# Two sixteen-head attention layers of a fused eight-layer kernel joined into one pipeline of sixteen batches

## The chip, the cores and the metric

The kernel runs on one core of a Trainium2 chip. The metric is the device time of one execution, in microseconds (us). Five engines work side by side, each on its own list of instructions in order: TensorE (PE in the rows, PEld for its weight loads), VectorE (DVE), ScalarE (ACT), GpSimd (POOL) and SyncE (SP), which here only issues DMA transfers. They meet at semaphores.

## The reference, cut to what matters

`x` is (8 batches, 256 tokens, 256 features). Eight layers follow one another; each adds its result to `x`. The two that the change touches are the third pair:

```python
x = x + _L2_xattn_ref(_layernorm(x), ctx_1024, ...)   # "a2": q from x, k and v from the context, biases
x = x + _L2_ffn_ref(_layernorm(x), ...)               # "f2": q, k and v from x itself, with a router
# inside _L2_ffn_ref, per head of 16 features:
q_norm = q / norm(q);  q_scaled = (q_norm + query_embedding) * softplus(temperature)
attn = softmax(q_scaled @ k.T / 4);  h = attn @ v
gates = softmax(h @ Wr.T + br)   # 15 experts, the three largest are summed, times 3
sw = softmax(h @ Ws.T + bs)      # 2 values
out = h * (2*sw[0]*sw[0] + 2*sw[1]*3*top3_sum);  return out @ Wp.T + bp
```

Both attentions work on each batch by itself: batch b of `f2` needs batch b of `x` after `a2`, and no other batch.

## The kernel before

`program` calls one function for each layer in the order a0, f0, a1, f1, a2, f2, a3, f3. `attention16` serves a0 (shared keys and values), a2 (`bias=True`) and f2 (`router=True, kv_from_x=True`). Each call opens a block of its own: it clears its semaphores, loads its weights, fills GpSimd's tiles `KP` and `v4` with ones, computes the layer-norm factors of all sixteen token tiles at once (`norm_factors` on VectorE, a square root on ScalarE), and then runs its steps. No engine enters the next block before all have left the last.

A step is a round over eight numbers n = 0..7. At each n come a `score` of the batch three behind, a `max` of the batch two behind, and then the extras of `HEAD_EXTRAS` (a2, a0) or `ROUTED_EXTRAS` (f2), each with the number of batches that it lags: the normalised rows transposed (`xT`), the projections `q`, `k`, `v`, the negated maxima transposed (`neg0`, `neg1`), weighing of values (`weigh0..3`), output transposes (`T0`, `T1`, `aT`) and the output projection `y`. With eight batches and a lag of five there are 13 steps for each layer; in the last five, no new batch enters. All engines walk the same lists. `HEAD_MOVES` and `ROUTED_MOVES` give the order in which SyncE issues the DMAs that carry q, k and the negated maxima through DRAM into `QP` and `KP`; it waits at each until its data is there. The small products share two PSUM buffers (`GP`, a ring in the order of the list), so the use of a buffer waits for whoever reads the use before the last.

`max` is four matmuls into two PSUM tiles `MX[0]` and `MX[1]`, and VectorE reduces each with an instruction of its own (line 806). `score` writes `EX`, which ScalarE turns into exponentials (line 558).

In f2 the query path is: `q` on TensorE, then `square` (bias, square and sum per head on VectorE), a power of -0.5 on GpSimd (line 498), `scale` (one Newton step, factor and embedding on VectorE), transposes `qT`, a split by ScalarE (line 525) and by GpSimd (line 483). The router is `gate` on TensorE, `gate_logits`, one exponential on ScalarE (line 573) and `gate_factor` on VectorE.

Of the kernel before, what the change touches and what calls it, by code (L numbers as in the profile page):

```python
# [20 lines left out]
P = 128  # L21
# [189 lines left out]

def add_to_x(dve, g, b, y):

    xb = g.x[:, bass.ds(b * TT, TT), :]
    op = dve.tensor_tensor(xb, xb, y, ALU.add)
    return op


def next_stats(dve, g, b):
    for t in range(TT):  # L220
        i = b * TT + t
        dve.bn_stats(g.stats[:, bass.ds(i, 1), :].rearrange("p a d -> p (a d)"),
                     g.x[:, bass.ds(i, 1), :].rearrange("p a d -> p (a d)"))
# [32 lines left out]
def at_least(eng, sem, count):  # L256
    if count > 0:
# [10 lines left out]
HEAD_MOVES = [("ctx", -1), ("neg1_out", 3), ("q_in", 1), ("neg1_in", 3), ("k_in", 1), ("q_out", 0), ("neg0_out", 2),  # L268
              ("k_out", 0), ("neg0_in", 2)]
ROUTED_MOVES = [("neg1_out", 3), ("k_in", 1), ("neg1_in", 3), ("q_out", 1), ("q_in", 1), ("neg0_out", 2), ("k_out", 0),  # L270
                ("neg0_in", 2)]


def head_steps(extras):

    steps = []
    for s in range(-1, B + LOOKAHEAD):
        step = []
        for n in range(H // 2):
            step += [(f"score{n}", s - 3), (f"max{n}", s - 2)]  # L280
            step += [(what, s - part) for what, part in extras.get(n, [])]
        steps.append([(what, b) for what, b in step if 0 <= b < B])
    return steps
# [6 lines left out]
def attention16(nc, g, name, w, kv_from_x=False, shared_kv=False, bias=False, router=False):  # L290
# [7 lines left out]
    steps = head_steps(ROUTED_EXTRAS if router else HEAD_EXTRAS)  # L298
    moves = [(what, s - part) for s in range(-1, B + LOOKAHEAD)
             for what, part in (ROUTED_MOVES if router else HEAD_MOVES)  # L300
             if 0 <= s - part < B and not (shared_kv and what in ("k_out", "k_in"))
             and not (kv_from_x and what == "ctx")]
# [3 lines left out]
    column = lambda h: 8 * (h // 8) + 4 * (h % 2) + (h // 2) % 4  # L306

    with ExitStack() as ctx:
# [6 lines left out]
        wq, wv, wo = sb("wq", [P, KD, D]), sb("wv", [P, KD, VH * 16]), sb("wo", [P, KD, D])  # L315
        wk = sb("wk", [P, KD, P if shared_kv else D])
        xn = sb("xn", [P, TT, D])
        xnT = sb("xnT", [P, KD, S])
        kvT2 = None if kv_from_x else sb("kvT", [P, 2, KD, S])
# [15 lines left out]
        bk = sb("bk", [P, KD])  # L335
        if bias:
            bq = sb("bq", [P, KD])
            bv, bo = sb("bv", [P, D]), sb("bo", [P, D])
        if router:
            bqt, qe = sb("bqt", [P, D]), sb("qe", [P, D])  # L340
            sp_t = sb("sp_t", [P, 4, H])
            spq = sb("spq", [P, H])
            half = sb("half", [P, TT * H])
            qtm, qsq = sb("qtm", [P, TT, D]), sb("qsq", [P, TT, D])
            qn = sb("qn", [P, 3, TT * H])
            wr, br = sb("wr", [P, KD, H + 1]), sb("br", [P, H + 1])
            lg, le = sb("lg", [P, TT, 24]), sb("le", [P, TT, 24])
            top, sm = sb("top", [P, TT, 8]), sb("sm", [P, TT, 8])
        ps = lambda n, k: [ctx.enter_context(nc.psum_tensor(f"{name}_{n}{i}", [P, TT, S], F32)) for i in range(k)]
        GP, MX, EX, OT = ps("gp", 2), ps("mx", 2), ps("ex", 2), ps("ot", 2)  # L350

        first_in, weights_in = sem("first_in"), sem("weights_in")
# [10 lines left out]
        q_sums, q_roots, q_scaled, softplus, act_step = (sem(n) for n in (  # L363
            "q_sums", "q_roots", "q_scaled", "softplus", "act_step"))
        gate_in, gate_exp = sem("gate_in"), sem("gate_exp")
        gp_full, gp_read = [sem(f"gp_full{i}") for i in range(2)], [sem(f"gp_read{i}") for i in range(2)]
        mx_full, mx_read = [sem(f"mx_full{i}") for i in range(2)], [sem(f"mx_read{i}") for i in range(2)]
# [15 lines left out]
        def scored(eng, b):  # L383
            eng.wait_ge(ex_full[1], 8 * (b + 1))

        row_of = lambda v: w[v].rearrange("(a n) -> a n", a=1)
        first_loads = [(wq[:], w["wq"].rearrange("(k p) n -> p k n", p=P)),
                       (wk[:], w["wk"].rearrange("(k p) n -> p k n", p=P)), (bk[:], w["bk"])]
        loads = [(wv[:], w["wv"].rearrange("(k p) n -> p k n", p=P)), (wo[:], w["wo"].rearrange("(k p) n -> p k n", p=P))]
        if bias:  # L390
            loads += [(bv[:], row_of("bv").broadcast_to([P, D])), (bo[:], row_of("bo").broadcast_to([P, D]))]
        if bias and not router:
            first_loads += [(bq[:], w["bq"])]
        if router:
            first_loads += [(bqt[:], row_of("bq").broadcast_to([P, D])), (qe[:], row_of("qe").broadcast_to([P, D])),
                            (sp_t[:, 0, :], row_of("temp").broadcast_to([P, H]))]
            loads += [(wr[:], w["wr"].rearrange("(k p) n -> p k n", p=P)),
                      (br[:], row_of("br").broadcast_to([P, H + 1]))]
        first_all, all_in = 16 * len(first_loads), 16 * len(loads)
# [5 lines left out]
        def _(sp):  # L405
# [3 lines left out]
            def load_rest():  # L409
                for dst, src in loads:  # L410
                    sp.dma_start(dst, src).then_inc(weights_in, 16)

# [37 lines left out]
            if kv_from_x:  # L450
# [21 lines left out]
        def _(pool):  # L472
            pool.memset(KP[:].bitcast(F32), 1.0).then_inc(fixed, 1)
            pool.memset(v4[:], 1.0).then_inc(fixed, 1)
            if router:
                pool.memset(half[:], -0.5)
                pool.drain()
# [8 lines left out]
            for step in steps:  # L486
                for what, b in step:
                    if what == "norm":
                        if b >= 1:
                            full(pool, "xT", b - 1)  # L490
                        normalise(pool, g, b, xn, xn_ready)
                    elif what == ("qT" if router else "q"):
# [3 lines left out]
                    elif what == "square":  # L496
                        pool.wait_ge(q_sums, b + 1)
                        pool.tensor_tensor(qn[:, 2], qn[:, 0], half[:], ALU.pow).then_inc(q_roots, 1)
                    elif what == "v" and bias:
                        if b == 0:  # L500
                            pool.wait_ge(weights_in, all_in)
                        pool.wait_ge(xn_ready, b + 1)
                        xb = g.x[:, b * TT:(b + 1) * TT, :]
                        pool.tensor_tensor(xb, xb, bo[:].rearrange("p (a n) -> p a n", a=1).broadcast_to([P, TT, D]),
# [3 lines left out]
        def _(act):  # L508
            norm_sqrt(act, g, sqrt_in, sqrt_out)
            act.wait_ge(first_in, first_all)  # L510
            if router:
# [19 lines left out]
            for step in steps:  # L531
                for what, b in step:
                    bank = gp.slot((what, b)) if (what, b) in gp.place else None
                    if what == "xT":
                        if kv_from_x and b >= 1:
# [3 lines left out]
                    elif what == "q" and not router:  # L539
                        split_rows("q", b, qf, qs, q_split, q_out, bq if bias else None)  # L540
                    elif what == "qT":
                        split_rows("qT", b, qf, qs, q_split, q_out, None)
# [2257 lines left out]
```

## Time and profile before

| | us |
|---|---|
| median of 3 runs | 2100.21 (2098.96 to 2108.5) |
| the profiled execution, its own time | 2091.46 |
| its span in the trace | 2089.7 |
| TensorE busy | 1607.8 |
| VectorE busy | 996.2 |
| ScalarE busy | 674.8 |
| GpSimd busy | 512.9 |

The rows below are of that one execution. Its own time is 8.75 us under the median of the runs. In the rows `a_` names a tile of an attention layer and `f_` one of an f layer; between 969.2 and 1507.7 us of the span these are a2 and f2. The granted clock of TensorE is a share of 2.4 GHz. A row of the windows gives the stretch and its length, then busy us with the count of instructions for PE, PEld, DVE, ACT and POOL, then the granted clock, the share of time the DMA engines were busy, and GB/s. In a timeline, a group of several instructions shows its start and its length, and in brackets how long the engine was idle before it, and for whom.

### The profile page before, as it was taken

The numbers are of one execution on the slowest core, as the hardware profiler recorded it, in microseconds if no ns is written. First come the engines' busy times: TensorE is split into PE (matmuls) and PEld (weight loads), VectorE is DVE, ScalarE is ACT, GpSimd is POOL, SyncE is SP. The second block draws the span as 40 slices with busy tenths as digits, with TensorE's granted clock in tenths as the row PEclk, the third lists the DMA queues.
The fourth block names the chain that finished last, engine by engine and source line by source line (L and its number), as shares of the span: only waits on it lengthen the run. The fifth ranks groups of instructions, "written<-read, shape, count | busy, mean of one in ns | idle before, by whom it ended". The sixth has DMA issues, their size and how long they took to land. (4 is left out here: it accounts for less than half of the span.)

```text
span 2089.7 us, 33375 instructions
## 1 busy us (share of the span) xinstructions
PE 1607.8 (77%) x12250; PEld 1235.2 (59%) x12250; DVE 996.2 (48%) x2190; ACT 674.8 (32%) x1408; POOL 512.9 (25%) x583
## 2 busy tenths in 40 slices
PE   4898775905888519981699746888699999999976
PEld 2565654804566418871466434655478888888766
DVE  2675262524454422113366446776426554455542
ACT  1464342302555101111366413434332222222111
POOL 2110043052444020005331064431042223222110
PEclk8798797957999659995799967988799999999986
DMA  4230553435644258852756034442110000000001
GB/s 135 68 83 18 185 213 105 135 91 153 141 112 92 75 204 295 301 197 86 166 130 133 3 85 108 103 92 53 44 55 7 6 7 1 6 6 2 1 7 41
DMA packets 89430, 195.54 MB, mean 94 GB/s; under 512 B 13536, under 2 KB 62176, under 8 KB 80704
## 3 DMA queue, kind: packets, MB, share of 16 engines
q1 hardware_dynamic: 76352, 173.07, 28.9%
q0 software_dynamic: 4608, 12.59, 1.8%
q10 hardware_dynamic: 8320, 7.87, 1.1%
q8 instruction: 96, 1.57, 0.3%
q14 instruction: 54, 0.44, 0.1%
HBM read 136.47 MB, written 57.02 MB: 93 GB/s over the span
## 5 line engine op out<-in xcount | busy, mean ns | idle before, releaser
L806 DVE TENSOR_REDUCE a_sb_mx<-a_mx 128x2 f32<-128x512 f32 x256 | 164.8, 686 | 97.7 <-PE a_mx L634 97.4
L1161 DVE RECIPROCAL a_sb_rden<-a_ot 128x256 f32<-128x256 f32 x64 | 112.1, 1752 | 146.6 <-PE a_ot L1047 146.5
L558 ACT ACTIVATE a_sb_probs<-a_ex 128x512 f32<-128x512 f32 x256 | 139.2, 598 | 103.9 <-PE a_ex L655 103.3
L230 PE MATMUL a_gp<-g_ident,a_sb_xn 128*128 128x128 f32 x128 | 25.1, 329 | 163.0 <-POOL a_sb_xn L206 80.0
L230 PEld LDWEIGHTS a_gp<-g_ident,a_sb_xn 128*128 128x128 f32 x128 | 16.9, 165 | 167.5 <-DMA a_sb_bo<-a_bo 70.9
L806 DVE TENSOR_REDUCE f_sb_mx<-f_mx 128x2 f32<-128x512 f32 x128 | 82.2, 684 | 36.7 <-PE f_mx L634 36.3
L558 ACT ACTIVATE f_sb_probs<-f_ex 128x512 f32<-128x512 f32 x128 | 69.5, 597 | 71.5 <-PE f_ex L655 71.4
L990 ACT ACTIVATE a_sb_probs<-a_sc 128x512 f32<-128x512 f32 x64 | 38.2, 597 | 167.9 <-PE a_sc L1035 111.7
L959 POOL TENSOR_SCALAR_AFFINE_SELECT a_sb_probs<-a_sb_probs 128x256 f32<-128x256 f32 x128 | 49.2, 409 | 164.9 <-ACT a_sb_probs L991 164.8
L655 PE MATMUL a_ex<-a_sb_QP,a_sb_KP 49*128 49x256 f32 x512 | 68.1, 343 | 24.8 <-ACT a_sb_probs L558 21.3
L952 POOL TENSOR_TENSOR a_sb_q_lo<-a_sb_whole,a_sb_q_hi 128x512 fp32r<-128x512 f32 x32 | 40.7, 1271 | 180.0 <-ACT a_sb_q_hi L981 180.0
L2488 PE MATMUL f_hb<-f_sb_xsT,f_sb_wb 128*128 128x128 f32 x640 | 76.0, 281 | 10.9 <-ACT f_sb_xsT L2441 10.9
L2488 PEld LDWEIGHTS f_hb<-f_sb_xsT,f_sb_wb 128*128 128x128 f32 x640 | 74.3, 196 | 13.1 <-issue 6.6
L980 ACT ACTIVATE a_sb_whole<-a_gp 128x512 f32<-128x512 f32 x64 | 38.3, 598 | 134.5 <-PE a_gp L999 134.5
L655 PEld LDWEIGHTS a_ex<-a_sb_QP,a_sb_KP 49*128 49x128 f32 x512 | 42.2, 197 | 63.9 <-issue 40.2
L634 PE MATMUL a_mx<-a_sb_KP,a_sb_QP 48*128 48x256 f32 x512 | 62.7, 322 | 17.4 <-DVE a_sb_mx L806 16.3
L668 PE MATMUL a_ot<-a_sb_probs,a_sb_v 128*32 128x256 f32 x1024 | 74.1, 410 | 0.0
L2602 DVE TENSOR_SCALAR f_sb_hT<-f_hb,f_sb_wb 128x128 f32<-128x128 f32 x80 | 22.5, 344 | 105.3 <-PE f_hb L2488 105.3
L1336 POOL TENSOR_SCALAR_AFFINE_SELECT a_sb_sim<-a_sb_sim 128x256 f32<-128x256 f32 x128 | 49.9, 418 | 89.0 <-ACT a_sb_sim L1390 89.0
L2497 PE MATMUL f_yb<-f_sb_wb,f_sb_hT 128*128 128x256 f32 x320 | 70.7, 379 | 0.0
L1146 DVE TENSOR_REDUCE a_sb_mx<-a_sc 128x2 f32<-128x256 f32 (+1 forms) x128 | 62.1, 544 | 11.6 <-PE a_sc L1020 11.6
L2497 PEld LDWEIGHTS f_yb<-f_sb_wb,f_sb_hT 128*128 128x128 f32 x320 | 60.0, 190 | 7.7
(427 smaller groups left out, 3929.5 us busy)
## 6 DMA issues: line engine op xcount, KB each, us to landing
f_sb_wb<-f_w SPq DMA_DIRECT2D x20, 2052.0 KB, 11.3
a_sb_kvT<-ctxT SPq DMA_DIRECT2D x32, 256.0 KB, 3.5
a_q_moved<-a_sb_qs SPq DMA_DIRECT2D x16, 512.0 KB, 3.5
a_sb_QP<-a_q_moved SPq DMA_DIRECT2D x32, 256.0 KB, 4.7
f_x_slots<-f_sb_zero SPq DMA_DIRECT2D x1, 6144.0 KB, 20.1
f_sb_xs<-f_x_slots SPq DMA_DIRECT2D x20, 256.0 KB, 2.8
f_y_slots<-f_sb_ys ACTq DMA_DIRECT2D x20, 256.0 KB, 2.6
a_sb_QP<-a_q_moved SPq DMA_DIRECT2D x32, 128.0 KB, 5.0
```

What stands on the lines that cost most here:

```text
L230: op = pe.transpose(out[:, k, t * P:(t + 1) * P], xn[:, t, k * P:(k + 1) * P], g.ident[:])
L558: act.activation(probs[:, group % 3, 2 * (u % 2) + par], EX[par][:], ACT.Exp, scale=scale)\
L634: op = pe.matmul(MX[par][:, t, :], QP[at:at + R, b % 3, u, t * P:(t + 1) * P], KP[at:at + R, b % KB, u % KM, :], start=True, stop=True)
L655: op = pe.matmul(EX[par][:, t, :], KP[at:at + R + 1, b % KB, u % KM, t * P:(t + 1) * P], QP[at:at + R + 1, b % 3, u, :], start=True, stop= ...
L668: op = pe.matmul(OT[c // 2][32 * j:32 * j + 32, c % 2, :], v4[:, b % 4, t, (4 * c + j) % VH, :], probs[:, (4 * b + c) % 3, j, t, :], start ...
L806: dve.tensor_reduce(mx[:, :, column(2 * u + par)], MX[par][:], AX.X, ALU.max, negate=True)\
L959: op = pool.affine_select(later, later, [[0, 2], [1, P]], ALU.is_ge, 0.0, base=0, channel_multiplier=-1)
L1146: op = dve.tensor_reduce(mx[:, t, 2 * i:2 * i + 2], SC[pair][:, :, t, 0:(t + 1) * P], AX.X, ALU.max, negate=True)
L1161: dve.reciprocal(rden[:, n], OT[n][:, 1, :])
L1336: op = pool.affine_select(later, later, [[0, 2], [1, P]], ALU.is_ge, 0.0, base=0, channel_multiplier=-1)
L2488: op = pe.matmul(HB[j % 2][c // (FC // 2)][:, c % (FC // 2), :], w1(j, k, c), xsT[:, j, k, :], start=(k == 0), stop=(k == KD - 1))
L2497: op = pe.matmul(YB[j % 2][:, 0], hT[:, j, c, :], w2(j, c), start=(c == 0), stop=(c == FC - 1))
```

## The change

`attention16` takes a list of layers and runs a2 and f2 as one pipeline of sixteen batches: batches 0 to 7 are a2's, 8 to 15 f2's. The weights of both have tiles of their own; f2's large ones are loaded behind a2's. `norm_factors` runs once, for a2. For batches 8 to 15 GpSimd computes the layer-norm factors itself, batch by batch (`batch_norm_factors`), after `y` of the batch eight before has given the new statistics.

```diff
-    elif s == "a2":
-        attention16(nc, g, s, w, bias=True)
-    elif s == "f2":
-        attention16(nc, g, s, w, bias=True, kv_from_x=True, router=True)
+    elif s == "a2":
+        layers = [(sub(io, n + "_"), n == "f2") for n in ("a2", "f2") if n in stages]
+        attention16(nc, g, s, layers)
```
```diff
+def batch_norm_factors(eng, g, b, ln):
+    at = slice(b * TT, (b + 1) * TT)
+    st = lambda i: g.stats[:, at, i]
+    eng.tensor_tensor(ln[:, 0, :], st(1), st(4), ALU.add)
...
+    root_guess(eng, g.rstd[:, at], ln[:, 3, :])
+    for _ in range(3):
+        root(eng, g.rstd[:, at], ln[:, 3, :], g.rstd[:, at], ln[:, 4, :])
```
`root_guess` is one operation on the bits, `root` four operations with a drain after each.
```diff
-ROUTED_EXTRAS = {0: [("neg1", 3), ("xT", 0), ("weigh3", 4), ("y", 5)], 1: [("q", 0), ("square", 0), ("out1", 4)],
-                 2: [("weigh0", 3), ("T0", 4), ("T1", 4)], 3: [("k", 0)], 4: [("neg0", 2), ("weigh1", 3), ("aT", 4)],
-                 5: [("scale", 0), ("gate", 4), ("v", 0), ("out0", 3), ("norm", -1)], 6: [("weigh2", 3), ("gexp", 4)],
-                 7: [("qT", 0), ("factor", 4)]}
+ROUTED_EXTRAS = {0: [("neg1", 3), ("xT", 0), ("weigh3", 4), ("y", 5)], 1: [("q", 0), ("out1", 4), ("norm", -1)],
+                 2: [("square", 0), ("weigh0", 3), ("T0", 4), ("T1", 4)], 3: [("k", 0), ("sums", 0)],
+                 4: [("neg0", 2), ("weigh1", 3), ("aT", 4), ("roots", 0)], 5: [("gate", 4), ("out0", 3)],
+                 6: [("weigh2", 3), ("gexp", 4), ("v", 0), ("scale", 0)], 7: [("qT", 0), ("factor", 4)]}
```
In a routed step the work moves so: the square goes from VectorE to ScalarE; the inverse root goes from one power on GpSimd and a Newton step on VectorE to fourteen small operations on GpSimd; adding the embedding becomes the bias of ScalarE's split of `qT`; the copies of the negated maxima go from VectorE to ScalarE.
```diff
-                        pool.tensor_tensor(qn[:, 2], qn[:, 0], half[:], ALU.pow).then_inc(q_roots, 1)
+                        root_guess(pool, qn[:, 3], qn[:, 0])
+                        for _ in range(3):
+                            root(pool, qn[:, 3], qn[:, 0], qn[:, 3], qn[:, 1])
+                        by_token = lambda a: a.rearrange("p (t h) -> p t h", t=TT)
+                        pool.tensor_tensor(by_token(qn[:, 2]), by_token(qn[:, 3]), ..., ALU.mult).then_inc(q_rooted, 1)
```
The router's exponential on ScalarE becomes six instructions, three for each token tile, each of which also gives the sum of its row; the three largest are found in the logits, before the exponential, and twelve small VectorE operations are left of nineteen.
```diff
-                        act.activation(le[:, :, 0:H + 1], lg[:, :, 0:H + 1], ACT.Exp).then_inc(gate_exp, 1)
+                        for t in range(TT):
+                            act.activation(le[:, t, 0:H - 1], lg[:, t, 0:H - 1], ACT.Exp, bias=neg_top[:, t, 0:1],
+                                           accum_out=sums[:, t, 0:1])
...
```
In all three layers served by `attention16`, a0 too, the two maxima tiles become one, which VectorE reduces with one instruction:
```diff
-                        for par in range(2):
-                            dve.wait_ge(mx_full[par], 8 * b + u + 1)
-                            dve.tensor_reduce(mx[:, :, column(2 * u + par)], MX[par][:], AX.X, ALU.max, negate=True)\
-                               .then_inc(mx_read[par], 1)
+                        dve.wait_ge(mx_full, 2 * (8 * b + u + 1))
+                        pair = mx[:].rearrange("p t (i g h) -> p g t i h", i=2, g=2)[:, :, :, u // 4, u % 4]
+                        dve.tensor_reduce(pair, MX[:], AX.X, ALU.max, negate=True).then_inc(mx_read, 1)
```
On SyncE, in a routed step, the second half of the negated maxima comes back (`neg1_in`) ahead of the keys (`k_in`) instead of behind them. Five small loads of f2 now stand in a2's first group, which the first q waits for.

## Rows read from the trace of the kernel before

**Rows 1.** Windows: a2 until its last batch enters, its tail, f2 likewise.
```profile
969.20:1136.60 167.40, 132.73 (x982) 91.76 (x982) 87.63 (x152) 81.50 (x168) 58.21 (x42) 0.87 0.58 139
1136.60:1205.20 68.60, 51.70 (x459) 32.10 (x458) 34.30 (x68) 31.66 (x59) 0.00 (x0) 0.89 0.14 25
1205.20:1421.80 216.60, 154.99 (x1038) 106.66 (x1038) 141.26 (x299) 80.56 (x159) 101.86 (x50) 0.79 0.40 96
1421.80:1507.70 85.90, 67.01 (x499) 42.22 (x498) 47.44 (x165) 33.34 (x65) 1.27 (x1) 0.80 0.12 26
```

**Rows 2.** Windows, same columns: one full step of a2, one full step of f2.
```profile
1115.40:1136.60 21.20, 20.35 (x181) 13.77 (x180) 14.13 (x26) 13.68 (x28) 3.78 (x3) 1.00 0.56 127
1391.60:1421.80 30.20, 26.42 (x193) 17.63 (x192) 21.75 (x57) 13.50 (x27) 9.24 (x4) 0.83 0.37 88
```

**Rows 3.** What TensorE waited for in f2: us in total, times, longest.
```profile
PE f_mx L634 <- DVE f_sb_mx L806: 27.7, 21, 4.5
PE f_gp L230 <- DVE f_sb_qtm L733: 18.1, 2, 9.1
```

**Rows 4.** Timeline of TensorE in a full step of f2: start, duration, what.
```profile
1383.40 1.06 PE L587 MATMUL f_gp<-f_sb_wr,f_sb_oT 128*128 128x17 f32 x8
1384.31 1.97 PE L587 MATMUL f_gp<-f_sb_wv,f_sb_xnT 128*128 128x256 f32 x8
...
1390.53 0.50 PE L634 MATMUL f_mx<-f_sb_KP,f_sb_QP 48*128 48x256 f32 x4 [1.99 <-DVE f_sb_mx L806]
1390.96 0.66 PE L230 MATMUL f_gp<-g_ident,f_sb_qtm 128*128 128x128 f32 x4
...
1397.03 3.78 PE L587 MATMUL f_gp<-f_sb_wo,f_sb_oT 128*128 128x256 f32 x8 [0.52 <-DVE f_sb_negT L813]
1400.74 0.80 PE L655 MATMUL f_ex<-f_sb_QP,f_sb_KP 49*128 49x256 f32 x4
```

**Rows 5.** Timeline of TensorE in a full step of a2.
```profile
1124.40 0.40 PE L634 MATMUL a_mx<-a_sb_KP,a_sb_QP 48*128 48x256 f32 x4
1124.73 1.99 PE L580 MATMUL a_gp<-a_sb_kvT,a_sb_wk 128*128 128x256 f32 x8
```

**Rows 6.** VectorE in f2, groups by shape: busy us, mean ns, idle before.
```profile
L806 DVE TENSOR_REDUCE f_sb_mx<-f_mx 128x2 f32<-128x512 f32 x128 | 82.2, 684 | 36.7 <-PE f_mx L634 36.3
L813 DVE CAST f_sb_negT<-f_gp 8x256 fp32r<-8x256 f32 x16 | 6.4, 403 | 0.1
L717 DVE TENSOR_TENSOR f_sb_qsq<-f_sb_qtm 128x512 f32<-128x512 f32 x8 | 5.5, 692 | 0.7
L1189 DVE TENSOR_TENSOR f_sb_qn<-f_sb_qn 128x32 f32<-128x32 f32 x8 | 4.0, 502 | 11.2 <-POOL f_sb_qn L498 11.2
L726 DVE TENSOR_TENSOR f_sb_qn<-f_sb_qn,f_sb_spq 128x32 f32<-128x32 f32 x8 | 1.6, 202 | 0.6
```

**Rows 7.** GpSimd in the whole span, groups by shape.
```profile
L498 POOL TENSOR_TENSOR f_sb_qn<-f_sb_qn,f_sb_half 128x32 f32<-128x32 f32 x8 | 43.6, 5454 | 69.7 <-DVE f_sb_qn L719 69.7
L483 POOL TENSOR_TENSOR f_sb_qs<-f_sb_qf,f_sb_qs 128x512 fp32r<-128x512 f32 x8 | 10.2, 1271 | 43.8 <-ACT f_sb_qs L525 43.8
L1932 POOL TENSOR_TENSOR f_sb_s_hT<-f_sb_s_act,f_sb_s_lin 128x256 f32<-128x256 f32 x8 | 6.3, 789 | 36.8 <-ACT f_sb_s_lin L2012 36.8
L476 POOL MEMSET f_sb_half<- 128x32 f32 x1 | 0.1, 143 | 0.0
```

**Rows 8.** ScalarE in f2, groups by shape.
```profile
L528 ACT ACTIVATE f_sb_ks<-f_gp,f_sb_bk 128x256 fp32r<-128x256 f32 x16 | 6.7, 480 | 0.0
L573 ACT ACTIVATE f_sb_le<-f_sb_lg 128x34 f32<-128x34 f32 x8 | 1.9, 234 | 5.5 <-DVE f_sb_lg L746 5.5
L558 ACT ACT_TABLE_LOAD x1 | 1.3, 1283 | 0.0
```

**Rows 9.** Timeline of VectorE at f2's start, beside GpSimd's memset.
```profile
1205.78 4.74 DVE L177 TENSOR_SCALAR g_ln_mean<-g_ln_mean 128x16 f32<-128x16 f32 x1
```

**Rows 10.** Timeline of SyncE's queue at f2's start, one of twelve loads.
```profile
1206.73 0.43 SPq L407 DMA_DIRECT2D f_sb_bqt<-f_bq  x1
```

More of the change, by code:

```diff
@@ L280, in head_steps, with __init__, attention16 @@
             step += [(f"score{n}", s - 3), (f"max{n}", s - 2)]
-            step += [(what, s - part) for what, part in extras.get(n, [])]
-        steps.append([(what, b) for what, b in step if 0 <= b < B])
-    return steps
+            for which, extras in ((True, ROUTED_EXTRAS), (False, HEAD_EXTRAS)):
+                step += [(what, s - part) for what, part in extras.get(n, []) if of_layer(s - part, which)]
+        steps.append([(what, b) for what, b in step if 0 <= b < n_b])
+        moves += [(what, s - part) for what, part, kinds in MOVES
+                  if 0 <= s - part < n_b and routed[(s - part) // B] in kinds]
+    return steps, moves
 def number(what):
     return int("".join(c for c in what if c.isdigit()))
-def attention16(nc, g, name, w, kv_from_x=False, shared_kv=False, bias=False, router=False):
+class Layer:
+    def __init__(self, i, w, router):
+        self.w, self.router, self.first = w, router, i * B
+def attention16(nc, g, name, layers, shared_kv=False):
     io = g.io
@@ L297, in attention16 @@
     scale = 0.25
[L298 to L302, printed above, removed]
+    bias = not shared_kv
+    L = [Layer(i, w, router) for i, (w, router) in enumerate(layers)]
+    NB = B * len(L)
+    of = lambda b: L[b // B]
+    routed = lambda b: of(b).router
+    steps, moves = head_steps([l.router for l in L])
+    moves = [(what, b) for what, b in moves if not (shared_kv and what in ("k_out", "k_in"))]
     flat = [u for step in steps for u in step]
@@ L392, in attention16 @@
[L392 to L399, printed above, removed]
+        by_k = lambda a: a.rearrange("(k p) n -> p k n", p=P)
@@ L748, in gate_logits @@
-                op.then_inc(gate_in, 1)
+                dve.tensor_scalar(neg_top[:, :, 0], top[:, :, 0], -1.0, None, ALU.mult)
+                dve.drain()
+                dve.sem_inc(gate_in, 1)
             def gate_factor(b):
-                dve.wait_ge(gate_exp, b + 1)
-                for i, (lo, hi) in enumerate(((0, H - 1), (H - 1, H + 1))):
-                    dve.tensor_reduce(sm[:, :, i], le[:, :, lo:hi], AX.X, ALU.add)
-                for t in range(TT):
-                    dve.max(top[:, t, :], le[:, t, 0:H - 1])
+                dve.wait_ge(gate_exp, b - of(b).first + 1)
@@ L776, in _ @@
                     bank = gp.slot((what, b)) if (what, b) in gp.place else None
-                    if what == "square":
-                        square_q(b)
+                    if what == "q" and routed(b):
+                        bias_q(b)
+                    elif what == "sums":
+                        sum_q(b)
                     elif what == "scale":
```

314 lines of the change are left out of this document (184 added, 130 removed).

## The prediction

> **What bounds it now.** I read the windows of the stretch first. From 969.2 us to 1507.7 us, 538.5 us, the chip works on the two layers, in four parts: a2 until its last batch is in (167.4 us), a2's tail of five steps in which no batch enters (68.6), f2 until its last batch is in (216.6), f2's tail (85.9) [rows 1]. The reader is to see TensorE: 52 us of work in a tail of 68.6, and 155 us in f2's 216.6, at a granted clock of 0.79. Everything outside this stretch stays as it is, but for a0, below.
>
> Then one full step of each layer [rows 2]. A step of a2 takes 21.2 us, and TensorE is busy for 20.35 of them at its upper level, 2.4 GHz all the way. This layer is bound by TensorE. A step of f2 takes 30.2 us. VectorE is busy for 21.75 of them, TensorE for 26.42, but at a mean clock of 0.83: part of that work ran at the lower level, 1.2 GHz.
>
> The waits say why. TensorE's largest wait in f2 is for the reduction of the maxima on VectorE, 27.7 us, and then for the scaled query [rows 3]. In the timeline of the step the 1.99 us before the max at 1390.53 are such a wait; VectorE was busy with Newton step, scaling, embedding and router in front of that reduction. Soon after it the clock is down: the output projection at 1397.03 takes 3.71 us to the next score, where a product of the same size takes 1.93 in a2 [rows 4, 5]. So f2 loses to VectorE's order of work, and then a second time by the clock.
>
> **Part 1, the join.** a2's tail and f2's start now overlap. Batch 8 needs the statistics of batch 0, which `y` gives in step 4; its `norm` is in step 7, three steps later, so nothing waits there. The stretch becomes: a2's first part as it is, 167.4; eight steps with routed batches entering; one tail of a routed layer. What is removed is 68.6 + 216.6 + 85.9 = 371.1 us [rows 1]; I now price what takes its place.
>
> **Part 2, a full routed step (steps 12 to 15).** TensorE: the 20.35 us of an a2 step, plus what only f2 has, the gate with 0.91 (1383.40 to 1384.31) and the transposes of q with 0.6 [rows 2, 4]: 21.9 us. With the 0.85 us that an a2 step already idles: 22.7.
>
> VectorE: of its 21.75 us it loses the square (0.69), the added embedding (the same shape, 0.69), two copies of negated maxima (0.81), and five small operations of Newton step and factor; these go from 0.20 to 0.50 each, 1.0 to 2.5 us, I take the middle, 1.75 [rows 6]. The router loses seven small operations of 0.15 to 0.20, about 1.2. That leaves 16.6 us for 24. The joined reduction saves nothing I can count: two of 0.684 that overlap against one of 1024 elements. If the element rate holds it costs about 1.2 instead of 1.3 us; if a reduction over two tiles gained nothing, 1.37. I take it as equal, here and in a0: 0.1 us either way on each of 64 pairs a layer is 6 us of VectorE's work in a layer, most of it in its idle time.
>
> Three waits are new or left. After the last `v` product, VectorE copies v and scales q (0.69 each, the shape of the square [rows 6]) and hands over twice (0.1 each), 1.6 us, before `qT` can start; TensorE has one score and one max in between, 0.33 each [rows 5]: 0.9 us idle. The next step's first max waits for the reduction behind that scaling: 0.25. Then `xT` waits for its PSUM buffer until ScalarE has written q twice, now with a bias and so in four instructions of 0.48 [rows 8], 1.6 us less the matmuls in between: 0.5. Sum 1.65, so the step is 22.7 + 1.65 = 24.3 us, if the clock stays up.
>
> Steps 8 to 11 have routed q work but no gate yet (it lags four): 22.7 - 0.9 + 0.9 = 22.7 us.
>
> **Part 3, GpSimd's small operations.** The trace has no short arithmetic on GpSimd. From below: a memset of 128x32 took 0.143. From above: a subtraction on 512 elements took 1.27, and one on 32 can't take more; the power with 5.45 is another operation. The nearest two-input rows are 0.789 for 256 and 1.27 for 512; their line gives 0.31 + 0.06 for 32, so 0.37 us [rows 7]. I take that, drain included. The chain that matters is in the middle of the step: ScalarE splits k in 1.5 us after TensorE's k, GpSimd takes 1.27 for the rest, then come fourteen root operations, 5.2 us, to 8.0. VectorE wants the result behind v. k closes n = 3 and v n = 6, so this is three eighths of a step later, 9.1. In total GpSimd has in a step the fourteen and 21 of `batch_norm_factors` (13.0 us), two for normalising and three for the splits and the bias, which I put at 1.27 each (6.3): 19.3 of 24.3. It is hidden, with 1.1 us to spare in the chain. At 0.45 us each the cover is gone and each further 0.1 us costs 1.4 us a step.
>
> The Trainium skill speaks against this part: its page Perfetto Trace Analysis, Optimizing GPSIMD Operations and the note on offloading, says to prefer other engines, because GpSimd and VectorE share an SBUF port, so that moving work between those two may not help. The trace has a case: a 128x16 operation of VectorE took 4.74 us beside a memset of GpSimd [rows 9]. What that would make of the sum is a rival below.
>
> **Part 4, the rest.** ScalarE takes on the square (0.6), two copies (0.4 each), five more instructions for the router (0.23 each, or up to 0.48 with the sums) and two more splits: 13.5 + 3 to 4.5, or at most 18 of 24 [rows 2, 8]; the six router exponentials stand behind score 6, beside weigh2 and v, 3 us of TensorE. Hidden; if not, 1 to 2 us a step. SyncE: `neg1_in` moves ahead of four issues of about 0.45; its data is needed at n = 4, ten us later, no gain; `k_in` needs to land before the next step. Nothing. At the start, five more loads in the first group (0.43 each, 2.2 us of queue [rows 10]) land while GpSimd fills its tiles: 0, at worst 2. The exponential and logarithm for softplus run in the same shadow.
>
> **Part 5, the tail.** It lies between a2's 68.6 and f2's 85.9 [rows 1]: gate and router are in it, the slow clock (0.80) and VectorE's excess partly not. I take the middle, 77.
>
> **Sum.** 4 x 22.7 + 4 x 24.3 + 77 = 265 us in place of 371.1: 106 us less. The profiled execution, 2091.5, would become 1985.5; the median of the runs, 8.75 us higher, becomes 2100.2 - 106 = 1994 us.
>
> **Rivals.**
> A. The clock falls in the routed steps as it does now. For it: bubbles of 0.9 and 0.5 us remain behind `v`, where 1.99 preceded the fall. Against: a0 and a2 keep 2.4 GHz with small waits. It costs what the slow piece costs now, about 3.3 us in steps 12 to 15 and 1.3 before them, and the tail is 86: 4 x 24 + 4 x 27.6 + 86 = 292, 79 less: 2021 us.
> B. GpSimd sets the step, with about 0.6 us for a small operation: 35 x 0.6 + 6.3 = 27.3, so 28 us with its waits; 8 x 28 + 86 = 310, 61 less: 2039.
> C. The port: what VectorE hands to GpSimd costs it as much in waits. 1.75 us a step come back on the path, 14 us in all: 2008.
> D. ScalarE has to exchange its function table for the square. The row of such a load is 1.283 [rows 8]; two in each routed step, half hidden: 10 us, 2004 to 2014. Copies and exponentials alternate without one now; for a square there is no row.
> E. Slower. A small GpSimd operation with its drain takes 1.27 us, as much as a large one. Then GpSimd needs 35 x 1.27 + 6.3 = 51 us a step: 8 x 51 + 86 = 494, 123 more: 2223. It decides from the point where a step reaches (371 - 86) / 8 = 35.6 us, 0.84 us for each operation. Speaking against it: the larger one has sixteen times the elements.
> F. Better than forecast: the waits hide and the tail is a2's. 8 x 22.7 + 68.6 = 250, 121 less: 1979.
>
> **How the numbers follow.** Forecast 0.48; A 0.18; B 0.08; C 0.08; D 0.05; E 0.03; F 0.10. Their neighbourhoods overlap. The predicted time is the forecast's, 1994. The range goes from F, lowered by the 8.75 us by which single executions differ, 1971, to just short of B, 2034; left out are E, most of B and what lies below F. 0.5% is 10.5 us, about what a measurement of this kernel can tell from no change. Only E, or a mishap I did not list, gives a time above 2090: slower 0.03, same 0.01, faster 0.96.
>
> **What would show it.** Between about 969 and 1402 us one stretch without a hole; steps 8 to 11 near 22.7 us and 12 to 15 near 24.3, at a clock of 1.0; the max waits of 2 us gone and one near 0.9 us before `qT`; small GpSimd operations spaced 0.3 to 0.4 us and the last root before VectorE's copy of v; a tail under 80 us. The forecast is wrong if VectorE waits for GpSimd before scaling, if GpSimd's spacing passes 0.45, if table loads appear behind squares, or if the clock in the routed steps is near 0.85.

## The result, and the profile after

| | before | changed |
|---|---|---|
| median, us | 2102.89 (2098.96 to 2108.5, 4 runs) | 1991.82 (1987.47 to 1997.49, 4 runs) |
| profiled execution, own time | 2091.46 | 1997.49 |
| its span | 2089.7 | 1995.7 |
| TensorE, VectorE busy | 1607.8, 996.2 | 1571.1, 942.9 |
| ScalarE, GpSimd busy | 674.8, 512.9 | 694.5, 523.9 |

The ratio is 0.9472 (95% interval 0.9437 to 0.9506): 104 to 118 us of 2102.9 are gone. The forecast was 1994. The two profiled executions lie on opposite sides of their medians, so that between the traces only 94 us are to be seen; a later trace of the same changed kernel (experiment 3) has a span of 1988.3, and so shows 101.

First the windows of the changed kernel, with the columns of [rows 1]: until a2's last batch is in, steps 8 to 11, steps 12 to 15, the tail (its last 0.6 us, in which TensorE is done, are left out); then step 9, step 10 and step 14 by themselves. Step 8 is the first in which a batch of f2 enters; steps 8 to 11 also carry the rest of a2, and step 14 is a full routed step.

```profile
969.20:1133.60 164.40, 130.79 (x982) 90.42 (x983) 85.22 (x107) 84.72 (x173) 68.10 (x83) 0.87 0.63 150
1133.60:1228.20 94.60, 84.16 (x739) 57.77 (x738) 66.51 (x81) 57.51 (x119) 49.70 (x142) 0.98 0.48 108
1228.20:1325.10 96.90, 89.75 (x761) 60.69 (x760) 68.13 (x120) 63.19 (x168) 47.99 (x137) 0.96 0.49 111
1325.10:1412.50 87.40, 67.48 (x499) 42.51 (x498) 40.20 (x108) 40.85 (x116) 1.28 (x1) 0.79 0.13 26
1156.80:1181.90 25.10, 22.29 (x187) 15.18 (x186) 17.01 (x21) 14.27 (x29) 15.25 (x44) 0.93 0.45 107
1181.90:1205.00 23.10, 20.58 (x185) 14.18 (x184) 16.69 (x20) 14.36 (x30) 11.93 (x37) 1.00 0.51 116
1274.90:1299.30 24.40, 22.33 (x195) 15.25 (x194) 17.49 (x33) 16.12 (x43) 13.65 (x40) 1.00 0.47 111
```

The stretch takes 443.9 us (969.2 to 1413.1) where it took 538.5, 94.6 less, which is the whole difference of the spans. The hole between the layers is gone, and the clock of the routed steps is 0.96 to 0.98 where it was 0.79 [rows 1]. The steps 8 to 15 are 23.2, 25.1, 23.2, 23.2, 21.4, 25.3, 24.4 and 25.8 us. VectorE is busy for 17.5 us of step 14, TensorE for 22.3 of 24.4. In f2's full step before, the two were 21.8 and 26.4 of 30.2 [rows 2]. TensorE now fills 92% of a full routed step with work at its upper clock level, where it filled 96% of a step of a2.

TensorE's waits of the changed kernel from 1133 to 1402 us (total, times, longest), to set beside [rows 3]:

```profile
PE a_ex L739 <- ACT a_sb_probs L639: 15.3, 21, 1.6
PE a_gp L252 <- DVE a_sb_qtm L810: 11.4, 8, 1.7
PE a_ot L752 <- ACT a_sb_probs L639: 2.1, 1, 2.1
PE a_mx L718 <- DVE a_sb_mx L880: 1.6, 2, 0.8
```

The wait for the maxima has gone from 27.7 us to 1.6. The wait for the scaled query was 18.1 us in two places; now there is one of about 1.4 us in every routed step. The largest total is now for ScalarE's exponentials; 10.0 of it lie between 1330 and 1412 us, in the tail.

TensorE's timeline in step 9 of the changed kernel, beside [rows 4], and behind it the end of step 8:

```profile
1172.62 1.99 PE L675 MATMUL a_gp<-a_sb_wv,a_sb_xnT 128*128 128x256 f32 x8
...
1175.88 0.40 PE L718 MATMUL a_mx<-a_sb_KP,a_sb_QP 48*128 48x256 f32 x4
1177.94 0.63 PE L252 MATMUL a_gp<-g_ident,a_sb_qtm 128*128 128x128 f32 x4 [1.65 <-DVE a_sb_qtm L810]
1178.40 3.53 PE L675 MATMUL a_gp<-a_sb_wo,a_sb_oT 128*128 128x256 f32 x8
```
```profile
1154.51 0.63 PE L252 MATMUL a_gp<-g_ident,a_sb_qtm 128*128 128x128 f32 x4 [1.38 <-DVE a_sb_qtm L810]
1154.97 1.89 PE L675 MATMUL a_gp<-a_sb_wo,a_sb_oT 128*128 128x256 f32 x8
```

The `y` (the output projection) at 1178.40 takes 3.53 us behind a wait of 1.65; in step 8 the same product takes 1.89 behind a wait of 1.38. The clock still falls here in steps 9, 13 and 15 (granted 0.93 over each of them, 1.00 over step 10), and stays at its upper level in the other five; step 12 has no `y` at all.

Near the end of step 12, VectorE first and then GpSimd in the same microseconds:

```profile
1247.01 0.69 DVE L871 TENSOR_TENSOR a_sb_v<-a_gp,a_sb_bv 128x512 f32<-128x512 f32 x1 [1.44 <-PE a_gp L675]
1247.62 1.26 DVE L810 TENSOR_TENSOR a_sb_qtm<-a_sb_qtm,a_sb_qn 128x512 f32<-128x512 f32 x1
1248.80 1.21 DVE L880 TENSOR_REDUCE a_sb_mx<-a_mx 128x4 f32<-128x1024 f32 x1
```
```profile
1246.08 0.22 POOL L1271 TENSOR_SCALAR a_sb_qn<-a_sb_qn 128x32 f32<-128x32 f32 x1 [0.16 <-issue]
1246.44 0.25 POOL L1273 TENSOR_TENSOR a_sb_qn<-a_sb_qn 128x32 f32<-128x32 f32 x1
1246.84 0.25 POOL L566 TENSOR_TENSOR a_sb_qn<-a_sb_qn,a_sb_spq 128x32 f32<-128x32 f32 x1
1247.05 1.28 POOL L573 TENSOR_TENSOR g_x_all<-g_x_all,a_sb_bo 128x512 f32<-128x512 f32 x1
```

The fourteen small operations of GpSimd start 0.36 to 0.42 us apart. The last of them ends at 1247.09, as VectorE begins its copy of v, and the scaling that needs it starts at 1247.62: in time, with 0.5 us to spare. Right behind it GpSimd starts a large operation, the output bias, and VectorE's scaling beside it takes 1.26 us, where the copy of the same shape, beside the same operation, took 0.69.

In steps 8 to 10 the roots are late instead: VectorE waits for them, three times, 1.5 us in all. The scaling of step 8, then GpSimd's addition beside it:

```profile
1152.62 1.75 DVE L810 TENSOR_TENSOR a_sb_qtm<-a_sb_qtm,a_sb_qn 128x512 f32<-128x512 f32 x1 [0.37 <-POOL a_sb_qn L566]
```
```profile
1152.54 1.28 POOL L573 TENSOR_TENSOR g_x_all<-g_x_all,a_sb_bo 128x512 f32<-128x512 f32 x1
```

Here the scaling takes 1.75 us, in step 12 it takes 1.26, and in both it ends 0.55 us behind the end of the addition.

### The profile page after: what moved, and what is told of

It is laid out like the page before. It is cut to its first block and busy times, and to the rows that moved or that the text cites. A ratio compares the mean times of both kernels' runs of the same rounds, so it can differ in the third digit from the quotient of the medians.

```text
span 1995.7 us, 33445 instructions
## 1 busy us (share of the span) xinstructions
PE 1571.1 (79%) x12250; PEld 1213.6 (61%) x12250; DVE 942.9 (47%) x1858; ACT 694.5 (35%) x1533; POOL 523.9 (26%) x852
## 3 DMA queue, kind: packets, MB, share of 16 engines
q1 hardware_dynamic: 76496, 172.94, 30.5%
## 5 line engine op out<-in xcount | busy, mean ns | idle before, releaser
L880 DVE TENSOR_REDUCE a_sb_mx<-a_mx 128x4 f32<-128x1024 f32 x192 | 234.7, 1223 | 114.9 <-PE a_mx L718 112.6
L639 ACT ACTIVATE a_sb_probs<-a_ex 128x512 f32<-128x512 f32 x384 | 208.8, 598 | 157.6 <-PE a_ex L739 157.3
L252 PE MATMUL a_gp<-g_ident,a_sb_xn 128*128 128x128 f32 x160 | 31.0, 325 | 165.3 <-POOL a_sb_xn L206 80.8
L739 PE MATMUL a_ex<-a_sb_QP,a_sb_KP 49*128 49x256 f32 x768 | 99.2, 335 | 32.3 <-ACT a_sb_probs L639 29.6
L752 PE MATMUL a_ot<-a_sb_probs,a_sb_v 128*32 128x256 f32 x1536 | 112.4, 414 | 2.1 <-ACT a_sb_probs L639 2.1
L739 PEld LDWEIGHTS a_ex<-a_sb_QP,a_sb_KP 49*128 49x128 f32 x768 | 61.0, 191 | 87.0 <-issue 58.0
L718 PE MATMUL a_mx<-a_sb_KP,a_sb_QP 48*128 48x256 f32 x768 | 90.4, 313 | 14.1 <-DVE a_sb_mx L880 13.3
L718 PEld LDWEIGHTS a_mx<-a_sb_KP,a_sb_QP 48*128 48x128 f32 x768 | 64.1, 201 | 25.6 <-DVE a_sb_mx L880 16.6
L539 POOL TENSOR_TENSOR a_sb_qs<-a_sb_qf,a_sb_qs 128x512 fp32r<-128x512 f32 x24 | 30.6, 1274 | 184.4 <-ACT a_sb_qs L594 97.2
L752 PEld LDWEIGHTS a_ot<-a_sb_probs,a_sb_v 128*32 128x32 f32 x1536 | 42.1, 114 | 40.1 <-issue 14.1
```

Source lines behind the costliest of these rows:

```text
L252: op = pe.transpose(out[:, k, t * P:(t + 1) * P], xn[:, t, k * P:(k + 1) * P], g.ident[:])
L639: act.activation(probs[:, group % 3, 2 * (u % 2) + par], EX[par][:], ACT.Exp, scale=scale)\
L718: op = pe.matmul(MX[:, par, t, :], QP[at:at + R, b % 3, u, t * P:(t + 1) * P], KP[at:at + R, b % KB, u % KM, :], start=True, stop=True)
L739: op = pe.matmul(EX[par][:, t, :], KP[at:at + R + 1, b % KB, u % KM, t * P:(t + 1) * P], QP[at:at + R + 1, b % 3, u, :], start=True, stop= ...
L752: op = pe.matmul(OT[c // 2][32 * j:32 * j + 32, c % 2, :], v4[:, b % 4, t, (4 * c + j) % VH, :], probs[:, (4 * b + c) % 3, j, t, :], start ...
L880: dve.tensor_reduce(pair, MX[:], AX.X, ALU.max, negate=True).then_inc(mx_read, 1)
```

## The experiments

Each was timed against the kernel before in the same series and on the same chip. There were three series: experiments 1 and 2 with the first run of 3 (median of the kernel before: 2099.82); the first run of 4 with all of 5, on another chip (2105.99); the second runs of 3 and 4 with 6, on the first chip again (2103.04). The changed kernel itself was timed in the first and the third; in the second only the ratio to the kernel before can be compared. The theory under test is the prediction's: the join fills the tail, and the rework of the routed step takes VectorE's excess away.

**1. The rework without the join, and the join without the rework.** In the first, the two layers stay two calls:

```diff
-                layers = [(sub(io, n + "_"), n == "f2") for n in ("a2", "f2") if n in stages]
-                attention16(nc, g, s, layers)
+                attention16(nc, g, s, [(w, False)])
+            elif s == "f2":
+                attention16(nc, g, s, [(w, True)])
```

> The changed routed steps, but a2 and f2 as two calls of the function, each with its own block, fill and tail. Theory (two parts, each worth something by itself): the steps of f2 that carry everything fall from 30.2 us to about 24.4, there are three or four such steps, and the maxima waits go: the stretch of the two layers becomes about 515 us from 538.5, the time about 2078 us, 20 to 30 us under the kernel before. Rival (the join is all of it, the rework only undoes what the join would have cost): within 5 us of the kernel before. Second rival (the rework is all of it and the join only hides a short fill): about 2010 us.

In the second, the routed step goes back to its old order and old owners inside the joined pipeline (square, Newton step, embedding, router and negated maxima on VectorE, the power on GpSimd, `neg1_in` behind `k_in`); GpSimd's `batch_norm_factors` and the joined reduction stay.

```diff
-                        root_guess(pool, qn[:, 3], qn[:, 0])
-                        for _ in range(3):
-                            root(pool, qn[:, 3], qn[:, 0], qn[:, 3], qn[:, 1])
...
+                        pool.tensor_tensor(qn[:, 2], qn[:, 0], half[:], ALU.pow).then_inc(q_rooted, 1)
```

> One pipeline of sixteen batches, but the routed step as it was: power on GpSimd, Newton step, square, embedding, router and copies of negated maxima on VectorE, old order of extras and of DMAs. Only the layer-norm factors per batch and the joined reduction stay from the change. Theory: steps with everything take 30 us as in f2 before, the four mixed ones about 24.5, the tail 86: the stretch is 164 + 219 + 86 = 469 us, about 70 us under the kernel before, so 2032 us. Rival (join is all): 1992 us, as the changed kernel. Rival (the join brings nothing without the rework): above 2080.

Measured: rework alone 2064.74 (ratio 0.9833, 0.9798 to 0.9868), 35 us gained, where 2078 was expected; join alone 2027.8 (0.9629, 0.9589 to 0.9669), 72 gained, where 2032 was expected. Both together gained 101 in the same series (2099.82 to 1998.95, experiment 3). The windows of f2 in the first:

```profile
1194.00:1470.90 276.90, 207.75 (x1536) 139.10 (x1536) 149.92 (x271) 136.14 (x353) 84.19 (x154) 0.84 0.36 83
```

and of the routed steps in the second:

```profile
1134.30:1354.00 219.70, 186.90 (x1496) 124.28 (x1496) 151.87 (x289) 106.37 (x210) 127.77 (x196) 0.91 0.42 96
```

f2 alone falls from 302.5 us (216.6 + 85.9 [rows 1]) to 276.9, its full steps from as much as 30.5 to between 22 and 26. The join alone leaves steps of up to 30.5 us, with VectorE busy for 151.9 of 219.7. So the two parts together pay nearly the sum of what each pays alone (101 against 107): one takes a tail away, the other shortens steps that are there in either case. Of the two, the join is worth twice as much.

**2. The router alone undone.** `gate_logits`, the one exponential and `gate_factor` as before, all else changed.

```diff
-                        for t in range(TT):
-                            act.activation(le[:, t, 0:H - 1], lg[:, t, 0:H - 1], ACT.Exp, bias=neg_top[:, t, 0:1],
-                                           accum_out=sums[:, t, 0:1])
...
+                        act.activation(le[:, :, 0:H + 1], lg[:, :, 0:H + 1], ACT.Exp).then_inc(gate_exp, 1)
```

> The changed kernel with the router part undone: one exponential on ScalarE, sums and maxima by small VectorE operations. Theory A (ScalarE is the waiting place in the tail): the six exponentials with their six accumulator reads hold ScalarE 1.7 us in front of the exponentials of score 7, where TensorE waits 1.63 us in each tail step against 0.71 in the kernel before, and then its clock falls; undone, the tail is 3 to 6 us shorter, steps 12 to 15 change by under 1 us each: 2 to 6 us faster than the changed kernel. Theory B (VectorE's seven saved operations carry the step): steps 12 to 15 get 1 to 1.5 us longer each, the kernel 4 to 6 us slower.

Measured 1994.12 (0.9488, 0.9455 to 0.9521), with steps of 23.2, 25.1, 23.2, 23.1, 21.5, 25.4 and 24.4, those of the changed kernel within 0.1. So theory B is refuted: seven small operations less on VectorE lie in its idle time. Theory A is not. The median is 4.8 us under that of the changed kernel in the same series (1998.95, experiment 3), inside the 2 to 6 us that it asked for, but the intervals of the two ratios overlap. The tail of the trace, all but its last 0.6 us:

```profile
1325.80:1407.50 81.70, 64.52 (x499) 41.11 (x498) 44.94 (x143) 35.19 (x72) 1.27 (x1) 0.79 0.13 28
```

TensorE is idle for 17.2 us of it, where it was idle for 19.9 in the changed kernel's at the same clock. The router's rework gained nothing, and may have cost some 3 us in the tail.

**3. The changed kernel again**, unchanged, in the first series and in the third.

> The changed kernel itself on the same chip, for the comparisons: 1992 us within 0.3%.

> The changed kernel on the same chip and in the same rounds, a third trace of its tail, which took 88.0 and 83.3 us in two: again between these if it is the clock's chance; 1992 us, a ratio near 0.949.

Measured 1998.95 (1990.17 to 2005.07), 0.35% above the 1992 expected, and 1993.73 (1991.29 to 1995.24), with stretches of 437.3 and 443.1 us. Steps 8 to 14 repeat within 0.1 us of the first trace. What lies behind them does not: in the first of these traces step 15 takes 24.3 us and the tail 83.3, in the second 25.8 and 88.0, as in the trace above. The tail of the shorter one:

```profile
1319.30:1402.50 83.20, 63.00 (x499) 40.44 (x498) 40.21 (x108) 41.18 (x116) 1.28 (x1) 0.82 0.13 27
```

TensorE is idle for 20.2 us of it, and for 19.9 us of the 87.4 above. What differs is how long the same 499 matmuls take, 63.0 against 67.5 us, at a clock of 0.82 against 0.79.

**4. The output bias later.** GpSimd's addition of the output bias moves, in routed steps, from `v` to behind its split of q, away from VectorE's scaling.

```diff
-                 6: [("weigh2", 3), ("gexp", 4), ("v", 0), ("scale", 0)], 7: [("qT", 0), ("factor", 4)]}
+                 6: [("weigh2", 3), ("gexp", 4), ("v", 0), ("scale", 0)], 7: [("qT", 0), ("factor", 4), ("bias", 0)]}
...
-                    elif what == "v" and bias:
+                    elif bias and what == ("bias" if routed(b) else "v"):
```

> The changed kernel with GpSimd's addition of the output bias moved, in routed steps, from right behind the roots to behind the split of q. Theory (shared port): the scaling of q on VectorE took 1.26 us instead of 0.69 because it ran beside that addition of 1.27 us; moved, the scaling takes 0.69 to 0.75, the wait before the transposes of q falls from 1.38 to about 0.8 us in eight steps, 4 to 5 us, and more if the clock then stays up in steps 9, 13 and 15: 1984 to 1988 us. Rival (the scaling is slow by itself, its access pattern has two strides): no change, 1992.

> The late bias again, with more rounds: its trace had the eight steps about 8 us shorter and the first part 4 us longer, where the code is the same. Theory (the first part's 4 us are a chance of where TensorE's clock falls in the fill): the first part is 164.4 again, the kernel 5 to 8 us under the changed one, a ratio to the kernel before of about 0.944. Rival (the later addition delays something there): the first part stays at 168.

Line 810, the scaling, in the first of these (nanoseconds: least, median, most), and TensorE at the end of step 12:

```profile
L810 DVE TENSOR_TENSOR a_sb_qtm<-a_sb_qtm,a_sb_qn x8: 681/681/694, 1150.2 to 1310.9; 128x512 f32<-128x512 f32 x8
```
```profile
1240.64 0.63 PE L252 MATMUL a_gp<-g_ident,a_sb_qtm 128*128 128x128 f32 x4 [0.80 <-DVE a_sb_qtm L810]
```

The same line in the changed kernel:

```profile
L810 DVE TENSOR_TENSOR a_sb_qtm<-a_sb_qtm,a_sb_qn x8: 1252/1320/1746, 1152.6 to 1323.2; 128x512 f32<-128x512 f32 x8
```

The median of the scaling falls from 1.32 to 0.68 us, and the wait from 1.38 to 0.80, in steps 8 to 10 to 0.6 or less; the steps 8 to 11 fall to 22.1, 22.4, 22.1 and 22.6. This shows that GpSimd's addition beside it is what stretched the scaling. How, the timelines of the changed kernel's three traces say: in all 24 scalings there the end lies 0.54 to 0.56 us behind the end of the addition, whether the scaling started 0.07 or 0.60 us after it. It looks like a wait until the addition is over, not like two operations that share a rate. In the total the gain is hard to see: 1991.84 against 1993.73 of the changed kernel, five executions of each (ratios 0.9471, 0.9454 to 0.9489, and 0.9481, 0.9463 to 0.9499), so 2 us, where 5 to 8 were expected. The stretch is 434.2 us in the second trace and 438.5 in the first, against 437.3 to 443.9 in the three of the changed kernel. In the first trace the part before step 8 took 168.2 us, with the clock at 0.84 instead of 0.87, and in the second 163.9, in the same code: that was chance. The earlier run gave 0.946 (0.9422 to 0.9497); it leaves out one execution of 4891.5 us, for which I have no explanation.

**5. Three single parts.** Two maxima tiles and two reductions again:

```diff
-                        dve.wait_ge(mx_full, 2 * (8 * b + u + 1))
-                        pair = mx[:].rearrange("p t (i g h) -> p g t i h", i=2, g=2)[:, :, :, u // 4, u % 4]
-                        dve.tensor_reduce(pair, MX[:], AX.X, ALU.max, negate=True).then_inc(mx_read, 1)
+                        for par in range(2):
+                            dve.wait_ge(mx_full[par], 8 * b + u + 1)
+                            dve.tensor_reduce(mx[:, :, column(2 * u + par)], MX[par][:], AX.X, ALU.max, negate=True)\
+                               .then_inc(mx_read[par], 1)
```

> The changed kernel with two maxima tiles and two reductions again. Theory: the joined reduction is what shortened a2's first part from 167.4 to 164.4 us, by 0.06 us of VectorE for each max where its wait stands on the path; undone, that part is 167 again, a0 gets 1 to 3 us longer, steps 8 to 15 up to 0.5 each: 5 to 9 us slower than the changed kernel. Rival (the first part got shorter by its start and the order of DMAs): no change within 2 us.

Its first part, with the columns of [rows 1]:

```profile
972.60:1140.20 167.60, 133.06 (x986) 91.93 (x988) 88.33 (x156) 84.62 (x173) 68.13 (x85) 0.87 0.62 147
```

167.6 us against 164.4, and a full step of a2 21.2 to 21.3 against 21.0: the joined reduction gives 3 us there. The part as a whole can move by 4 us without a cause in the code (experiment 4), but the full steps don't: the last four before step 8 are 21.2 to 21.3 us in both traces with two tiles and 21.0 in those with one, the last three of them even in that odd trace. Steps 8 to 15 did not get longer: 190.3 us, where the changed kernel took 189.8 to 191.5. The total, 2003.14 (0.9507, 0.9475 to 0.9538), overlaps with the changed kernel's; a time doesn't resolve it.

The negated maxima copied by VectorE:

```diff
-                    elif what.startswith("neg") and not routed(b):
+                    elif what.startswith("neg"):
```

> The changed kernel with the copies of the negated maxima of f2 back on VectorE. Theory: two copies of 0.40 us a step on an engine busy for 17 of 24, in places (n = 0 and 4) where TensorE has long products: under 1 us a step either way, and ScalarE is freed by 0.37 in the tail; within 4 us of the changed kernel. Rival (VectorE is the bound of the routed step): 0.8 us a step and the clock, 8 us slower or more.

Measured 1997.4 (0.9481, 0.9449 to 0.9513), steps as in the changed kernel: worth nothing that can be measured.

Five Newton steps on GpSimd for the roots of q, eight more operations in the chain that was just in time:

```diff
-                        for _ in range(3):
+                        for _ in range(5):
                             root(pool, qn[:, 3], qn[:, 0], qn[:, 3], qn[:, 1])
```

> The changed kernel with five Newton steps for the root of q on GpSimd instead of three, eight small operations more. Theory (the roots end just when VectorE wants them): 8 x 0.38 = 3.0 us later, of which the copy of v hides 0.5 at most; the wait before the transposes of q grows from 1.38 to about 3.9 us, the clock falls more often: 8 x 2.5 = 20 us or more, 2012 to 2025 us. Rival (GpSimd has slack, the wait is v's copy and the scaling alone): no change.

Measured 2035.04 (0.9665, 0.9619 to 0.9711), beyond the 2012 to 2025 expected, with TensorE's waits from 1130 to 1460 us headed by

```profile
PE a_gp L252 <- DVE a_sb_qtm L810: 34.9, 8, 4.8
```

4.4 us in each routed step for 1.4. The eight operations at 0.38 us are 3.0, less 0.5 of slack; the scaling adds 0.4, since it now starts together with the output bias each time and takes 1.73 us. The eight steps grow by 4.6 us each in the mean (228.2 us for 191.5), so 1.7 us a step come on top of the wait; the slower clock (0.89 over these steps for 0.97) is part of it, how much was not separated. With a slack of 0.5 us at most, the price is 1.5 times what is added (4.6 for 3.0).

Inside the joined pipeline the whole rework was worth 29 us (2027.8 against 1998.95). The router and the copies of the negated maxima have no measurable share in that. Square, roots, embedding and the order of extras and DMAs were undone only all together, and which of them carries the gain is not shown.

**6. The scaling ahead of v**, with the late output bias of experiment 4; VectorE waits there for the roots before it copies v.

```diff
-                 6: [("weigh2", 3), ("gexp", 4), ("v", 0), ("scale", 0)], 7: [("qT", 0), ("factor", 4)]}
+                 6: [("weigh2", 3), ("gexp", 4), ("scale", 0), ("v", 0)], 7: [("qT", 0), ("factor", 4), ("bias", 0)]}
```

> The late bias of the run before, and VectorE scales q ahead of its copy of v instead of behind it. Theory: the roots end as v's product ends, so the scaling starts 0.5 us earlier; the wait before the transposes of q falls from 0.80 to about 0.25 us, steps 12 to 15 to 23.2, the clock stays at 2.4 GHz in all eight; the stretch behind a2's first part is 4 us shorter than with the late bias alone, 10 to 12 shorter than in the changed kernel: 1981 to 1986 us. Rival (the roots are the bound now): the wait moves to VectorE and v's copy with it, no gain over the late bias alone.

TensorE at the end of step 12 of it:

```profile
1240.62 0.63 PE L252 MATMUL a_gp<-g_ident,a_sb_qtm 128*128 128x128 f32 x4 [0.29 <-DVE a_sb_qtm L810]
```

Measured 1987.54 (1982.16 to 1989.45; 0.9449, 0.9428 to 0.9469), stretch 431.1 us. All five executions lie under the changed kernel's five in that series (from 1991.29). It is the fastest version found, 6 us or 0.3% under the changed kernel by the medians; the intervals of the ratios just overlap. It stays short of the 1981 to 1986 us expected. About 2 us of what the shorter wait gives is taken back: the wait for the maxima is now 3.9 us in all, for 1.6. And the clock did not stay up in all eight steps: steps 9 and 10 took 23.4 us each at 0.93.

## Why the prediction was right

- **The join, right.** A tail and a start taken away; alone it gives 72 us. Nothing waits where the layers meet: in steps 8 to 11 TensorE's only listed waits are for the scaled query and for ScalarE's exponentials.
- **The first part, 164.4 for 167.4.** "I take it as equal" was wrong here. The joined reduction takes 1.22 us where the pair takes two of 0.69, and a2 has use for the difference, 0.2 to 0.3 us in each full step (experiment 5), although VectorE is idle for a third of such a step. That `max` waits for the reader of its tile is the likely way, but the list of waits of a full step of a2 names no wait for it.
- **Steps 8 to 11, 22.7 forecast; 23.2, 25.1, 23.2, 23.2.** The wait before the transposes was put at 0.9 and is 1.38 or more: the scaling was priced at 0.69 without its neighbour. Experiment 4 shows the 0.58 us. This is rival C's mechanism at a third of the price that the rival gave it. The Trainium skill, GPSIMD Engine Reference, Specifications, gives GpSimd's SBUF interfaces as shared with VectorE, with contention for VectorE operations that have two SBUF inputs. The trace agrees: the scaling has two and is stretched, the copy of v has one and PSUM, and takes 0.69. TensorE also waits 1.2 us a step for ScalarE's exponentials (4.7 us in the four), for which the sum had nothing but a2's idle time of 0.85; and in step 9 the clock falls.
- **Steps 12 to 15, 24.3 forecast; 21.4, 25.3, 24.4, 25.8.** The mean, 24.2, is right, but by errors that cancel. Step 12 is short because it has no `y`: a2's list has it at the end of the step four later, f2's at the start of the step five later, and the sum left that out. Steps 13 and 15 are long because the clock falls behind the wait that ends the step before them. And of the three waits in the sum, 0.9, 0.25 and 0.5, the first is 1.4 us, while the other two hardly came: no wait for the maxima before the tail, and 0.7 us in all behind `xT`'s buffer.
- **Rival A in part.** Three of eight steps (in one trace two) still lose the clock, 1.4 to 1.7 us of TensorE's time each. The wait ahead of `y` is 1.38 before step 13, which loses the clock, and 1.38 in step 8, which keeps it: the wait alone doesn't decide, and what does stays open. With the late bias and no wait there at all, step 9 kept the clock in one trace (22.4 us) and lost it in the other (23.4 us), where the product of `v` took 3.68 us behind a wait of 1.00 for ScalarE.
- **The tail, 88.0 for 77 (83.3 in one trace of three), the largest error.** The middle between a2's and f2's tail was taken as if the fall of the clock came from VectorE's excess. That excess is gone (40 us busy of 87), and the tail is f2's still: 20 us idle, where f2's had 18.9 and a2's 16.9 [rows 1], and the rest is matmuls at a clock of 0.79. A tail under 80 us, which the prediction named as a sign of being right, came in no trace. TensorE's largest wait there is for ScalarE's exponentials; that too few batches are in flight to fill the gap is argued. A reader can check one such wait; ScalarE's timeline of the changed kernel,

```profile
1346.55 0.31 ACT L655 ACTIVATE a_sb_le<-a_sb_lg,a_sb_neg_top 128x15 f32<-128x15 f32 x1
1346.75 0.20 ACT L655 ACTIVATION_READ_ACCUMULATOR a_sb_le<-a_sb_lg,a_sb_neg_top 128x1 f32 x1
...
1348.16 0.19 ACT L659 ACTIVATION_READ_ACCUMULATOR a_sb_le<-a_sb_lg,a_sb_neg_top 128x1 f32 x1
1348.25 1.06 ACT L639 ACTIVATE a_sb_probs<-a_ex 128x512 f32<-128x512 f32 x2
```

and TensorE's behind it:

```profile
1349.46 0.80 PE L739 MATMUL a_ex<-a_sb_QP,a_sb_KP 49*128 49x256 f32 x4 [1.63 <-ACT a_sb_probs L639]
```

  The router's six exponentials hold ScalarE for 1.70 us, and the next score waits 1.63. Without them (experiment 2) the tail was 82.3, just under the 83.3 to 88.0 of the changed kernel, with 2.7 us less idle time than the trace above at the same clock. So the router may explain some 3 us, and not the 11. That the low clock follows from the many small waits is argued, not shown, and experiment 5's second run speaks against it in this simple form: there TensorE was idle for 22.8 us of the tail's 85.0, more than in the other tails, and the clock was 0.84. Why the tail was 6 to 11 us longer than forecast stays open beyond that.
- **GpSimd, right in the price, wrong in the cover.** 0.37 us for a small operation, drain included; 0.38 measured for those on 32 elements, 0.34 on 2. But of the spare of 1.1 us only 0.5 was there in steps 11 to 15, and none in steps 8 to 10, where VectorE waited for the roots, 1.5 us in three waits. That was one of the signs by which the prediction would call itself wrong; TensorE's wait behind it, 1.38 to 1.65 us, is hardly longer than in the other steps. Experiment 5's added steps were paid one and a half times over. Rivals B and E had a real mechanism, as that run shows, and a wrong price.
- **Table loads, none.** The square runs between copies and exponentials at 0.63 us, and the only table load of the stretch is the one at its start; D falls.
- **The sum.** 106 us forecast; 94.6, 101.2 and 95.4 in the stretch of the three traces; 111 between the medians of the first timing, and 101 and 109 between those of the two series of experiment 3. The stretch came out 5 to 11 us longer than forecast, above all in the tail; the mechanism was right, and the term of the sum that was mis-sized is the tail. That the median was hit within 3 us owes something to the spread between executions: the profiled execution of before was quicker than all four timed ones, and a0, which has the joined reduction too, took 212 to 215 us in the changed kernel's three traces against 217, so 2 to 5 us may come from there. With the two tiles back (experiment 5) it took 214 as well, so that the joined reduction does it is not shown.

## What to carry to other kernels

Two pipelined layers that work batch by batch are worth joining: the gain is one fill and one tail less, and it adds to what a shorter step gives. When work moves to an engine whose chain ends just in time, price the neighbour too: what that engine does next runs beside the reader of its result, and can hold it up. Don't average a tail from its neighbours; count its waits and its idle time, since fewer batches in flight make every hand-over visible.

## What the runs showed of the hardware

- A drained chain of small GpSimd operations costs 0.38 us for each on 128x32 and 0.34 on 128x2, so fourteen of them, 5.3 us, cost what the one power of 5.45 us did.
- A VectorE operation on 128x512 with both inputs in SBUF takes 0.68 us alone and 1.23 to 1.75 beside a two-input GpSimd operation of 1.28 that started before it: it ends 0.55 us behind that operation, whenever it started. One with an input in PSUM took 0.69 beside it.
- A ScalarE activation of 2 to 15 elements with a sum of its row is two instructions, 0.29 and 0.19 us long, and the pair takes 0.28 us of its time.
- One VectorE reduction of 1024 PSUM elements in each of 128 partitions takes 1.22 us, two of 512 take 0.69 each.
- With the same program the clock in the tail was 0.82 in one execution and 0.79 in two, 4.5 us of matmul time.
